# Four graph-attention layers on one core: norm passes moved between engines, ELU computed in the accumulator banks, two layers' fp16 casts on ACT, other order weights

## Time and profile before

| | us |
|---|---|
| timed runs | 3186.02, 3187.56, 3191.8 (median 3187.56) |
| profiled execution, span from first to last instruction | 3188.3 |
| PE busy | 2872.0 (90%) |
| ACT busy | 2720.5 (85%) |
| DVE busy | 2654.2 (83%) |
| POOL busy | 2497.3 (78%) |
| DMA queue 1, share of 16 DMA engines | 56.9% |

### The profile page before, as it was taken

The page is one execution under the profiler, slowest core; times in us unless marked ns, Lnnn a source line. Parts: engine busy times, 40 slices in busy tenths (PEclk is TensorE's granted clock), DMA queues, the critical chain, the costliest instruction groups (busy, mean ns, idle before and its releaser), DMA issues. The chain is left out here.

```text
span 3188.3 us, 69772 instructions
## 1 busy us (share of the span) xinstructions
PE 2872.0 (90%) x22768; PEld 1557.5 (49%) x22768; DVE 2654.2 (83%) x7356; ACT 2720.5 (85%) x5847; POOL 2497.3 (78%) x2519
## 2 busy tenths in 40 slices
...
GB/s 148 97 69 106 121 103 109 144 125 120 130 112 121 117 137 126 120 125 111 134 114 142 125 126 105 124 138 104 147 123 119 106 139 127 120 120 100 100 114 86
DMA packets 1215802, 378.90 MB, mean 119 GB/s; under 512 B 1157712, under 2 KB 1194320, under 8 KB 1215440
## 3 DMA queue, kind: packets, MB, share of 16 engines
q1 hardware_dynamic: 1213616, 373.46, 56.9%
...
q10 hardware_dynamic: 1824, 0.99, 0.2%
...
## 5 line engine op out<-in xcount | busy, mean ns | idle before, releaser
L855 POOL TENSOR_TENSOR split_r<-prob_r,split_r 128x512 f16<-128x512 f32 x768 | 930.7, 1224 | 214.8 <-DVE split_r L1297 214.7
L1262 DVE CUSTOM_DVE_ANT_0 unused<-bank_ps,neg_mask 128x512 bf16<-128x512 f32 x1024 | 650.1, 682 | 47.6 <-PE bank_ps L1461 43.8
L1526 PE MATMUL bank_ps<-val_r,trans_r 128*128 128x64 f16 (+1 forms) x9216 | 626.1, 221 | 47.1 <-DMA trans_r<-split_r 46.6
L1084 ACT ACTIVATE prob_r<-bank_ps 128x512 f32<-128x512 f32 x1024 | 566.4, 601 | 118.9 <-PE bank_ps L1478 115.2
L1526 PEld LDWEIGHTS bank_ps<-val_r,trans_r 128*128 128x128 f16 x9216 | 522.1, 98 | 296.0 <-issue 122.3
L1247 DVE CUSTOM_DVE_ANT_0 masked_r<-bank_ps,neg_mask 128x512 f32<-128x512 f32 x768 | 508.1, 680 | 127.2 <-ACT bank_ps L1050 98.1
L1297 DVE CAST split_r<-prob_r 128x512 f16<-128x512 f32 x768 | 534.8, 703 | 88.5 <-ACT prob_r L1062 80.0
L1062 ACT ACTIVATE prob_r<-masked_r,low_r 128x512 f32<-128x512 f32 x768 | 557.4, 734 | 56.4 <-DVE low_r L1247 38.5
L1486 PE MATMUL bank_ps<-prob_r,value_ones 128*64 128x512 f32 (+1 forms) x2048 | 552.8, 610 | 2.7 <-ACT prob_r L1084 2.5
L1477 PE MATMUL bank_ps<-stack 98*128 98x512 f16 x1024 | 394.6, 385 | 55.9 <-DVE low_r L1247 19.7
L861 POOL TENSOR_TENSOR split_r<-xcur,split_r 128x512 f16<-128x512 f32 x256 | 300.2, 1186 | 130.6 <-ACT split_r L976 129.9
...
## 6 DMA issues: line engine op xcount, KB each, us to landing
stack<-qk SPq DMA_DIRECT2D x384, 128.0 KB, 2.6
...
trans_r<-split_r SPq DMA_TRANSPOSE x768, 2.8
...
stack<-low_rows SPq DMA_DIRECT2D x128, 4.0 KB
...
```

The costliest lines, as they stand in the source:

```text
L855: nc.gpsimd.tensor_tensor(split_r[:, j, 1, :], prob_r[:, i, :], split_r[:, j, 0, :], ALU.subtract).then_inc(lo_done.sem, 1)
L1084: nc.scalar.activation(prob_r[:, entry("prob", "pt", g, *key), :], bank_ps[entry("bank", "u", g, *key)][:], ACT.Exp).then_inc(exp_done.sem, 1)
L1262: nc.vector.tensor_tensor_reduce(out=unused[:, nth % 2, :], in0=bank_ps[entry("bank", "sq", g, t, b, h)][:], in1=neg_mask[:, b, :], scale= ...
L1526: ins = nc.tensor.matmul(bank[:, at:at + width], trans_r[:, i, pp, jb, :], val(g, layer)[:, vp, jb, cols], start=(n == 0), stop=(n == len( ...
```

## The change

- The norm passes `ap` of layers 0, 2, 3 and out are now one POOL instruction per block, (x - mean) * scale, with mean and scale as per-partition operands. `rs` is one POOL instruction (power -0.5); the addition of epsilon is a small DVE instruction in `nm`, behind a wait for the aggregate.
- The norms 1 and ffn have no pass of their own. `gain` and `skip`, `gain2` and `sum2` are on DVE, 128 x 256 each: (x - mean) * gain row, then times scale plus bias row (or plus x). The split for f1 reads the output of `skip`; the weights of f1 are no longer scaled by the gain.
- ELU: in layers 0 and 2 the Exp is written back into the accumulator bank, the division of layer 2 too, and `em` and `es` read the bank. The z tiles b0 and b2 are gone; the banks are held until `em` (layer 0) or `es` (layer 2).
- The fp16 cast of the probabilities is on ACT in layers 0 and 3 (`hi_a`) and stays on DVE in layer 2. `hid_hi` is on ACT and reads the bank with a second Relu.
- The planner's costs follow, `LEAD` is 106.0, and `LATER` is a new table with a weight for nearly every kind.

```diff
+    HIGH = {0: "hi_a", 2: "hi_v", 3: "hi_a"}
...
-              "q_hi": "act", "mr": "act", "ue": "act", "oc": "act", "fo": "act", "el": "act", "ap": "act",
-              "xt_lo": "dve", "job_lo": "dve", "hid_hi": "dve", "mk": "dve", "hi_v": "dve",
+              "q_hi": "act", "mr": "act", "ue": "act", "oc": "act", "fo": "act", "el": "act",
+              "hi_a": "act", "hid_hi": "act", "xt_lo": "dve", "job_lo": "dve", "mk": "dve", "hi_v": "dve", "gain": "dve", "skip": "dve", "gain2": "dve", "sum2": "dve",
               "nd": "dve", "mx": "dve", "mh": "dve", "ml": "dve", "rp": "dve", "dp": "dve", "rc": "dve", "dv": "dve",
               "em": "dve", "es": "dve", "st": "dve", "nm": "dve",
-              "lo": "pool", "hid_lo": "pool", "q_lo": "pool", "add": "pool", "gain": "pool", "skip": "pool", "shift": "pool",
-              "gain2": "pool", "sum2": "pool", "rs": "pool", "x_lo": "pool"}
+              "lo": "pool", "hid_lo": "pool", "q_lo": "pool", "add": "pool", "shift": "pool", "rs": "pool",
+              "ap": "pool", "x_lo": "pool"}
...
+    LATER = {"add_0": 12, "add_1": -57, "add_3": 72, "ap_0": 63, "ap_2": 97, "ap_3": -28, "ap_out": -5, "bc": 52, "bt": -52,
...
+    AP_US = 1.0
+    LEAD = 106.0
...
-            before = {0: [("load", g)], 1: halves("ap", 0), "ffn": halves("ap", 1), 2: halves("ap", "out"),
+            before = {0: [("load", g)], 1: halves("ap", 0), "ffn": [("skip", g, p) for p in range(HALF)], 2: halves("ap", "out"),
...
-                task(("job_hi", *key), 0.57, [("job", *key)] + [("gain", g, p) for p in range(HALF)], closes=[entry])
-                task(("hid_hi", g, n), 0.85, [("job_hi", *key)], opens=[("proj", (g, "f"))])
+                task(("job_hi", *key), 0.57, [("job", *key)])
+                task(("hid_hi", g, n), 0.57, [("job_hi", *key)], opens=[("proj", (g, "f"))], closes=[entry])
...
-            task(("hi_v", *key), 0.64, [("ex", *key)], opens=[("split", key)])
-            task(("lo", *key), 1.22, [("hi_v", *key)], closes=[("prob", key)])
+            task((HIGH[layer], *key), {"hi_v": 0.64, "hi_a": 0.52}[HIGH[layer]], [("ex", *key)], opens=[("split", key)])
+            task(("lo", *key), 1.16, [(HIGH[layer], *key)], closes=[("prob", key)])
...
-            task(("nm", g, which), 0.3, halves("st", which))
-            task(("rs", g, which), 2.1, [("nm", g, which)])
+            task(("nm", g, which), 0.45, halves("st", which))
+            task(("rs", g, which), 1.3, [("nm", g, which)])
+
+        def spread_out(which):
             for p in range(HALF):
-                task(("ap", g, which, p), 0.99, [("rs", g, which)], opens=[("z", (g, "b3"))] if which == 3 else [],
-                     closes=[("z", (g, {0: "a0", 2: "a2", 3: "a3", "out": "b1"}[which]))] if which in (0, 2, 3, "out") else [])
+                task(("ap", g, which, p), AP_US, [("rs", g, which)], opens=[("z", (g, "b3"))] if which == 3 else [],
+                     closes=[("z", (g, {0: "a0", 2: "a2", 3: "a3", "out": "b1"}[which]))])
...
-                    task(("em", g, layer, p), 1.0, [("fo", g, layer, p)], closes=[("z", (g, "b0"))])
+                    task(("em", g, layer, p), 0.61, [("fo", g, layer, p)], closes=[entry])
                     task(("add", g, layer, p), 1.27, [("em", g, layer, p)])
                 elif layer == 2:
-                    task(("el", g, p), 0.53, [("dv", g, layer, p)], opens=[("z", (g, "b2"))])
-                    task(("em", g, layer, p), 0.75, [("el", g, p)])
-                    task(("es", g, p), 1.15, [("em", g, layer, p)], closes=[("z", (g, "b2"))])
+                    task(("em", g, layer, p), 0.61, [("dv", g, layer, p)], opens=[("z", (g, "a2"))])
+                    task(("el", g, p), 0.5, [("em", g, layer, p)])
+                    task(("es", g, p), 0.61, [("el", g, p)], closes=[entry])
...
+        for p in range(HALF):
+            task(("gain", g, p), 0.80, [("rs", g, 1)])
+            task(("skip", g, p), 0.80, [("gain", g, p)], opens=[("z", (g, "b1"))])
...
-            task(("gain2", g, p), 1.27, [("ap", g, "ffn", p)])
-            task(("sum2", g, p), 1.45, [("gain2", g, p), ("shift", g, p)])
+            task(("gain2", g, p), 0.80, [("rs", g, "ffn")])
+            task(("sum2", g, p), 0.80, [("gain2", g, p), ("shift", g, p)])
         norm("out", lambda p: ("sum2", g, p))
+        spread_out("out")
...
+            if kind == "job" and key[1] == "f1":
+                return hidden_hi.at(key[0], key[2])
             if kind == "job":
-                return dense_hi.at(*key) if key[1] in ("f1", "v") else dense_lo.at(*key)
-            return scaled.at(*key) if key[1] in (0, 3) else divided.at(*key)
+                return dense_hi.at(*key) if key[1] == "v" else dense_lo.at(*key)
+            return {0: elu_max.at, 2: lambda g, _, p: elu_sum.at(g, p), 3: scaled.at}[key[1]](*key)
...
-                    nc.gpsimd.tensor_scalar(offset[s][:], moments[s][:, :, 0], -1.0, None, ALU.mult)
-                    nc.gpsimd.tensor_scalar(scale[s][:], moments[s][:, :, 1], EPS, None, ALU.add).then_inc(rsqrt_chain, 1)
-                    links += 1
-                    pool.wait_ge(rsqrt_chain, links)
-                    nc.gpsimd.tensor_tensor(scale[s][:], scale[s][:], exponent[:], ALU.pow).then_inc(rsqrt_chain, 1)
-                    links += 1
-                    pool.wait_ge(rsqrt_chain, links)
-                    nc.gpsimd.tensor_tensor(offset[s][:], offset[s][:], scale[s][:], ALU.mult).then_inc(norm_done.sem, 1)
+                    nc.gpsimd.tensor_tensor(scale[s][:], moments[s][:, :, 1], exponent[:], ALU.pow).then_inc(norm_done.sem, 1)
                 else:
-                    p, = key
-                    pool.wait_ge(*gained2.at(g, p))
-                    pool.wait_ge(*shifted.at(g, p))
-                    nc.gpsimd.tensor_tensor(z(g, "b1")[:, pair(p), :], z(g, "b1")[:, pair(p), :], xcur[s][:, pair(p), :],
-                                            ALU.add).then_inc(summed2.sem, 1)
+                    which, p = key
+                    pool.wait_ge(*norm_done.at(g, which))
+                    if which == 3:
+                        was = prior("z", g, "b3")
+                        if was is not None:
+                            pool.wait_ge(*z_free(was))
+                    src, dst = z(g, NORM_SRC[which]), (z(g, "b3") if which == 3 else xcur[s])
+                    for b in (2 * p, 2 * p + 1):
+                        ins = nc.gpsimd.tensor_scalar(dst[:, b, :], src[:, b, :], moments[s][:, b, 0:1], scale[s][:, b:b + 1],
+                                                      ALU.subtract, ALU.mult)
+                    ins.then_inc(applied.sem, 1)
...
+                elif kind == "hid_hi":
+                    n, = key
+                    act.wait_ge(*dense_done.at(g, "f1", n))
+                    was = prior("proj", g, "f")
+                    if was is not None:
+                        act.wait_ge(*proj_free(*was))
+                    nc.scalar.activation(proj(g, "f")[:, n, 0, :], bank_ps[entry("bank", "job", g, "f1", n)][:], ACT.Relu,
+                                         bias=ffn_bias[:, n:n + 1], scale=1.0 / WSCALE).then_inc(hidden_hi.sem, 1)
+                elif kind == "hi_a":
+                    unit = (g, *key)
+                    was = prior("split", *unit)
+                    if was is not None:
+                        act.wait_ge(*split_free(was))
+                    act.wait_ge(*probs_done.at(*unit))
+                    nc.scalar.copy(split_r[:, entry("split", *unit), 0, :],
+                                   prob_r[:, entry("prob", *unit), :]).then_inc(hi_act.sem, 1)
...
-                            ins = nc.scalar.activation(z(g, "b0")[:, b, :], acc, ACT.Exp, scale=by)
+                            ins = nc.scalar.activation(acc, acc, ACT.Exp, scale=by)
...
-                    nc.scalar.activation(z(g, "b2")[:, pair(p), :], z(g, "a2")[:, pair(p), :], ACT.Exp).then_inc(elu_exp.sem, 1)
-                    src = z(g, NORM_SRC[which])
-                    dst = z(g, NORM_DST[which]) if which in NORM_DST else xcur[s]
-                    for b in (2 * p, 2 * p + 1):
-                        ins = nc.scalar.activation(dst[:, b, :], src[:, b, :], ACT.Identity,
-                                                   bias=offset[s][:, b:b + 1], scale=scale[s][:, b:b + 1])
-                    ins.then_inc(applied.sem, 1)
+                    act.wait_ge(*elu_max.at(g, 2, p))
+                    bank = bank_ps[entry("bank", "acc", g, 2, p)]
+                    nc.scalar.activation(bank[:], bank[:], ACT.Exp).then_inc(elu_exp.sem, 1)
...
+                    nc.vector.scalar_tensor_tensor(out=flat(z(g, f"a{layer}")[:, pair(p), :]),
+                                                   in0=bank_ps[entry("bank", "acc", g, layer, p)][:], scalar=edge,
+                                                   in1=flat(other[:, pair(p), :]), op0=op, op1=ALU.add).then_inc(elu_max.sem, 1)
...
```

(28 more changed lines are left out.)

147 lines of the change are left out of this document (56 added, 91 removed), and 25 rows, old and new, of the table LATER.

## The result

The changed kernel takes 3321.34 us (median of 4 runs, 3318.49 to 3327.16) against 3189.68 us of the kernel before on the same chip: a ratio of 1.041, 95% interval 1.0394 to 1.0426. Forecast were 3088 us and a range up to 3220.

The account below looks back on a forecast made before the run. The prediction took a ring of queues with few buffers, paced by its heaviest feeder (ACT before, DVE after), as the bound. Pace 94.3 to 91.3 us over 32 graphs gives -96, order -4: 3188 to 3088 us, range 2985 to 3220.

Parts of the forecast that it names:

- POOL's pass: 512 norm passes of 128x256 moved to POOL: 0.50 us each (0.47 to 0.75), +256; POOL's net -246 us.
- the rule of the sum: Ring of queues: heaviest feeder, DVE at 82.8 us per graph, sets the pace at 91.3 us; -96 us over 32 graphs.
- The share: How full the ring gets a feeder: 90.7%, ACT's densest stretch, now taken for DVE; at 0.893 the time is 3133 us.
- ACT: Loses norm passes (-401.0), gains casts of layers 0 and 3 (+155) and second Relu (+45): net -201, 2519 us busy.
- DVE: Loses casts, gains gain, skip, gain2, sum2: net +34 us (-33 to +140), 82.8 us per graph.
- The ELU steps from the bank: DVE's 192 ELU steps with the bank as one input: 0.677 us each, 130 in all, -53 us.
- The new instructions: DVE's 512 for gain, skip, gain2, sum2, two SBUF inputs: 0.55 us each (0.42 to 0.75), +282 us.
- The addition of epsilon: One 128x4 DVE instruction per norm, 192 at 0.15 us: +29 us, plus +19 for waiting on its own aggregate.
- The order: New weights, graph distance 95.5 to 106 tasks: drain -8 us, half put against for start and worse fit, -4 in all.
- A: DVE's new instructions and POOL's passes wait for each other: DVE 86.1 us per graph, pace 96.4, 3255 us; chance 0.15.
- B: PE becomes the only bound, new instructions cost 0.42 us: pace 88.4 us per graph, 3000 us; chance 0.17.
- C: Loads fall, time doesn't; buffers, DMA transpose latency and fixed order hold the pace: 3160 to 3215 us; chance 0.15.

Follow-up runs that it names:

- e5: Changed kernel, same queue order, POOL's norm passes over 48 of 256 columns: 3142.91 us, 0.9861 of the kernel before.
- e6: Changed kernel, same queue order, DVE's gain, skip, gain2 and sum2 over 32 of 256 columns: 3253.19 us, 1.0202 of the kernel before.
- e10: Changed kernel, same queue order, POOL's norm passes cut to 48 columns and DVE's gain to sum2 to 32: 3039.55 us, 0.953 of the kernel before.
- e1: Changed kernel, same queue order, constants in place of the two per-partition operands of POOL's norm passes: 3255.91 us, 1.0194 of the kernel before.
- v1: Changed kernel, norm passes of layers 0, out and 2 back on ACT, epsilon added on POOL, measured prices, searched table: 3114.86 us, 0.9741 of the kernel before.
- c1: Kernel before, its work and prices unchanged, with order weights and graph distance found by a search over its plan: 3175.84 us, 0.9939.
- e9: Changed kernel with the graph distance 95.5 of the kernel before instead of 106, all weights kept: 3537.69 us, 1.1089 of the kernel before.
- e7: Kernel before with the order weights and graph distance of the changed kernel, nothing else: 3291.63 us, 1.0324.
- e4: Changed kernel with the order weights and graph distance (95.5) of the kernel before: 3629.02 us, 1.1368 of the kernel before.
- c2: Changed kernel's work with measured prices in the plan and a table found by the same search: 3226.08 us, 1.0095 of the kernel before.

## Why the prediction was wrong

**The step that failed, first: POOL's pass** in the part on POOL: "I take 0.50, near the low end, since it is the row with one input." The bounds were 0.47 and 0.75, and it measured 1.25 on the mean (638.2 / 512): +382 us of POOL, where POOL's whole net was to be -246 and came out at +86. The low end came from affine selects, another operation whose only likeness is the one input; the high end from the slope of TENSOR_TENSOR. Neither bounds a TENSOR_SCALAR, which costs more per element than both. The trace of before had no wide TENSOR_SCALAR on POOL, only 128 x 4 ones at 0.252. An honest upper end would have had to say that such a row has no slope in it. e5 shows that this term decides which way the time goes: at a pass of 0.57 us the same kernel in the same order is 1.4% faster than before. The sentence of the Trainium skill ("GPSIMD Engine Reference", "Performance versus the Vector engine") that a body of up to two operations goes at 1.03 cycles per element, an estimated 0.0009 us at the 1.2 GHz of its example, doesn't hold for these instructions: the measurement is 0.0033 us per element.

**The step that failed, second: the rule of the sum,** that the pace is set by the heaviest of the feeding engines, DVE, and POOL costs nothing beside it. With the right price POOL comes to 69.8 + 382 / 32 = 81.7 us per graph, still below DVE's 82.8, and the sum would have stayed at 3088, or 3133 with DVE's share at 0.893: still faster. The runs show another thing. POOL, the lighter of the two (82.1% of the even stretch against 88.7%), has 30% of the chain that ended last. Taking 353 us of busy time from POOL (2583.0 to 2230.4) gives 178 us (e5), taking 108 from DVE gives 68 (e6): half a us or a little more for each us, on either engine. The pace against the cost per graph (share of the even stretch times pace):

| run | DVE, us | POOL, us | pace, us |
|---|---|---|---|
| forecast | 82.8 | 69.8 | 91.3 |
| after | 85.8 | 79.3 | 96.7 |
| e6 | 82.3 | 78.9 | 94.9 |
| e5 | 86.3 | 68.4 | 91.8 |
| e10 | 82.1 | 67.9 | 88.5 |

So both engines count, the lighter one too, and POOL had the larger miss. Whether it is POOL's load or the delay of its pass in front of the split of x that counts isn't shown; ACT's wait for it, 163.6 us, fell to 109.2 in e1 and 11.0 in e5, and that delay is nowhere in the forecast.

The share was wrong as well: I held DVE to 90.7% of the stretch as what a feeder can reach; e5 has it at 94.0% and v1 at 95.3%. That 91.8 came out in e5 nevertheless, against 91.3, is luck, two errors against each other: DVE had more work, and was held less.

**ACT** was right in its terms: 154.8 us for the casts (155), 44.0 for the second Relu (45), the passes gone, 2534.7 in all (2519); the rest of the 16 us is spread over many rows.

**DVE** was 102 us too low. The ELU steps from the bank came out as priced (43.8 a group, three groups 130). The new instructions cost 306.3 us of busy time against 282 (0.60 each, above my 0.55). The addition of epsilon is the largest miss: 91.5 against 29, because a 128 x 4 instruction with a shortest of 0.169 us has a mean of 0.477. It reads and writes SBUF while POOL is at work, and L1200, from which I had its price, reads a bank. The casts kept their waits, 366.4 against 340. By the "SBUF — State Buffer" page of the Trainium skill ("Who interferes with whom") a tensor_scalar between SBUF tiles can take both ports and is held off by POOL, and the tail of L1373 fits that; no run changes only where this instruction reads. A part of DVE's busy time belongs to the order and not to the work: the kernel before has 2654.2 us, and with another table (c1) 2747.0.

**The order** I had at -4 us. It wasn't small: e9, e7 and e4 give 100 to 300 us for a table that doesn't fit its plan, and c2 gives back 95. I read the 106 as a shorter drain; the distance between graphs has no such meaning by itself. In the start, 41 to 71 us were lost in e5, e10, v1 and the changed kernel. Of the 71 us of the changed kernel e5 gives back 25 with the short pass. Why the first graph leaves later isn't shown beyond that; the new table alone delays it by 22 us in the kernel before (e7), and the old distance doesn't help (e9).

**The rivals.** A gave a number near the result, 3255, and more of it came true than its price. DVE's cost per graph, 85.8 us, is nearly A's 86.1, and at A's share of 0.893 it gives a pace of 96.1, next to the measured 96.7. The means of the four new rows, 0.803, 0.714, 0.605 and 0.497, average 0.65, just above the 0.64 that I had named as its sign, while their busy time is 0.60 each, since they overlap. But A's cause, that the ring holds DVE to such a share, is wrong: in e5 DVE costs 86.3 us per graph and the pace is 91.8. Two slips stand in A: by its own price of 0.75 DVE grows by 34 + 384 - 282 = 136 us, not 140, which moves its pace by 0.1; and tails are not absent at one input, the cast L1297 in the earlier trace rows goes up to 1.592. B's pace is what e10 reaches. C's main claim, that the loads fall and the time doesn't, is refuted in a fixed order by e5 and e10; that the order matters it had right.
